# Gated feed-forward kernel: one unit of the up stage stays in PSUM, the product stage has 11 units instead of 12, and two roundings of the sigmoid move to POOL

## The chip, the cores and the metric

The program runs on one core of a Trainium2 chip. Times are device microseconds (us) of that core; lower is better. The kernel before was timed in three runs, and one further execution was recorded by the profiler. The words unit, half and bank are explained below.

## What is computed

Input are four sequences of 1024 tokens with 256 values each, a context of 154 rows for each sequence, and weights. After an attention block comes a feed-forward block with 768 hidden values, and it is this block that the change touches. All of its intermediate results are rounded to a grid whose step is the largest absolute value of the whole tensor divided by 32767, so that no rounding can start before the last value of its tensor is known:

```python
def act_qdq(x):
    scale = jnp.maximum(jnp.max(jnp.abs(x)) / qmax, 1e-12)
    return jnp.clip(jnp.round(x / scale), -qmax - 1.0, qmax) * scale
...
x = act_qdq(x)
up = act_qdq(x @ lpbq_dequant(w_up).T)
gate = act_qdq(x @ lpbq_dequant(w_gate).T)
sig = fixed_qdq_u16(jax.nn.sigmoid(gate))
gate = act_qdq(gate * sig)
o = act_qdq(gate * up)
return o @ lpbq_dequant(w_down).T
```

## The kernel before, in words

Every engine has its own list of instructions, written out by hand, and waits on semaphores (`wait_ge`) that other engines raise (`then_inc`). Nothing reorders them: the order in which the code is written is the order in which each engine works.

The hidden tensor is 768 x 4096 (hidden values x tokens). It is cut in 12 **units** of 128 hidden values x 2048 tokens; unit u has hidden block k = u // 2 and token half u % 2. PSUM is used as two halves, `ps[0]` and `ps[1]`, of four banks each; a unit fills one half, a bank takes 512 tokens. TensorE (PE) makes one unit with 24 matmuls (`hidden_unit`, lines 740 to 759): four banks, each from `xh` and `xl` (the high and low part of the rounded input) and the high and low weights. A unit may be started when the PSUM half is free (`half_free[0]`, `half_free[1]`), and `unit_ps` tells that it is complete.

The feed-forward block runs in four stages:

- **Gate stage.** PE makes the 12 gate units, ScalarE (ACT) copies them to `hid`, VectorE (DVE) takes the largest value. The overall largest gives scale 2.
- **Up stage.** PE makes the 12 up units, but only their largest value is taken (`up_max`, line 1450) and the unit is dropped, because the scale of `up` is not yet known and 12 more units in float32 have no room. In the same time the gate is worked on, unit by unit: integer gate `gq` (by ACT, POOL and once DVE), sigmoid and absolute value (ACT), the sigmoid rounded to 16 bits, `sq` (`sigmoid_int`: DVE for unit 0 and all odd units, POOL for the even ones from 2 on), and the product of both with its largest value (`gated_max`, line 1461, on DVE). At the end DVE forms scale 3 (of `up`) and scale 4 (of the gated gate). For both, POOL takes the largest value over the partitions (`over_all`, line 479).
- **Product stage.** PE makes the 12 up units a second time. For each, ACT writes the rounded absolute value `au` and the rounded gated value `pq`, and DVE multiplies the sign of the unit in PSUM into `gq` (`product_sign`, line 1486; it raises `half_free`) and multiplies `pq` and `au`, with the largest value (`product_max`, line 1493). The last unit is taken bank by bank and in two parts. Then DVE and POOL form scale 5.
- **Down stage.** 16 chunks of 256 tokens are rounded, split in high and low parts, multiplied with the down weights and added to the residual. 24 matmuls whose result is not used (`WARM`) run ahead of it while the last scale is formed.

What sets the order around the change: DVE works strictly through `up_max(u)`, the rounding of u where it is DVE's, `gated_max(u)`; POOL's rounding of unit u waits for `p_rdy` >= u, that is until `gated_max(u - 1)` is done, since it writes over `sq[0]`; `half_free` after `up_max` lets PE go on two units later. ACT's first `au` waits for scale 3, its first `pq` for scale 4. PE is always ahead by up to two units, as there are two PSUM halves.

The buffers `ag`, `sq[0]` and later `au`, `pq[0]` share one region of 12288 bytes, and `sq[1]` and `pq[1]` the region of the gate weights.

Of the kernel before, what the change touches and what calls it, by code (L numbers as in the profile page):

```python
# [38 lines left out]
P = 128  # L39
# [27 lines left out]
def build(nc, x, ctx, g_xattn, g_ffn, w_sim, b_sim, w_qv, b_qv, w_gate, w_up, w_down, out):  # L67
# [61 lines left out]
    au = place(a, "au", [P, 2, HALF], I16)  # L129
    pq = [place(a, "pq0", [P, HALF], I16), place(copy_of(r_wg), "pq1", [P, HALF], I16)]  # L130
# [56 lines left out]
    gmx, umx, pmx, omx = col(NU + 3), col(NU), col(NU), col(NU + 1)  # L187
# [25 lines left out]
    with ExitStack() as stack:  # L213
# [41 lines left out]
        gbank_ps, ubank0_ps, ubank_ps, aubank_rdy = map(sem, ("gbank_ps", "ubank0_ps", "ubank_ps", "aubank_rdy"))  # L255
# [34 lines left out]
        WARM = 24  # L290
        HC = P + D
# [20 lines left out]
        def down_ps(par):  # L312
            return ps[0][:, par * (CD // P):(par + 1) * (CD // P), 0:D]
# [19 lines left out]
        def _(sp):  # L333
# [21 lines left out]
            sp.wait_ge(unit_ps, 3 * NU)  # L355
# [25 lines left out]
        def _(pool):  # L381
# [115 lines left out]
            for u in range(2, NU, 2):  # L497
                sigmoid_int(u)
                if u + 3 < NU:
# [6 lines left out]
        def _(pe):  # L506
# [254 lines left out]
            def hidden(wh, wl, done, first, bank_ps, bank0_ps=None):  # L761

                with pe.Fori(0, KF - 1) as k:
# [56 lines left out]
            pe.wait_ge(half_free[0], 3 * KF + 1)  # L820
            for i in range(WARM):
                pe.matmul(ps[0][:, i % 4, :], wdh[:, 0, 0:P], wdl[:, 0:2, :].rearrange("p k n -> p (k n)"), start=True, stop=True)
# [11 lines left out]
        def _(act):  # L834
# [785 lines left out]
```

## Time and profile before

| what | value |
|---|---|
| median of 3 runs | 461.97 us (461.82 to 462.2) |
| profiled execution, its own time | 459.6 us |
| span of its profile, first to last instruction | 457.8 us |
| mean granted clock of PE | 0.992 of full speed |
| PE busy in the span | 433.4 us (95%) |
| DVE busy | 363.4 us (79%) |
| ACT busy | 274.6 us (60%) |
| POOL busy | 110.7 us (24%) |
| gate stage on PE ends at | 260.4 us |
| up stage on PE | 260.4 to 322.7 us |
| product stage on PE | 322.7 to 385.8 us |
| down stage, first real matmul to the end | 392.0 to 457.8 us |

How to read it: times within the profile count from the first instruction. A row of a timeline has the start, the duration, the engine, the line of the code, the operation with its output and input, and in brackets the idle time before it and who ended that. Instructions that follow each other at once on DVE or ACT overlap in the record by up to 0.1 us, so the pitch from start to start is a little shorter than the duration. The time beyond the span (459.6 against 457.8 us) lies around the first and the last instruction.

### The profile page before, as it was taken

Reading aid. Unit: us, or ns where it says so; the run is one execution under the profiler, and the core shown is the slowest. Engines: PE = TensorE matmul, PEld = TensorE weight load, DVE = VectorE, ACT = ScalarE, POOL = GpSimd, SP = SyncE. Lnnn points to the kernel's source line nnn. Section 1 sums busy time; section 2 is a strip of 40 time slices with the busy share of each in tenths; the row PEclk is TensorE's granted clock in tenths of the full one; section 3 lists DMA queues with packets and bytes.
Section 4 is the critical chain, followed back from the end, with each engine's and each line's share of the span. In section 5 each row is a group of like instructions: output and inputs, shape, how many; then the busy total and the mean of one; then the engine's idle time right before and its main releaser. Section 6 shows DMA issues by size and latency. Waiting matters only on the chain.

```text
span 457.8 us, 6771 instructions
## 1 busy us (share of the span) xinstructions
PE 433.4 (95%) x2432; PEld 297.2 (65%) x2432; DVE 363.4 (79%) x652; ACT 274.6 (60%) x346; POOL 110.7 (24%) x109
## 2 busy tenths in 40 slices
PE   4899999999997698999999999999999999999997
PEld 3788898889876586744444444444444444788886
DVE  6786789797777488886433789999998889898874
ACT  2677365556525023284334599999296779987760
POOL 1239274365744453100000013334100000000000
PEclk9999999999999799999999999999999999999999
DMA  7950002000200020110000000000000000344442
GB/s 242 314 166 0 1 2 92 1 0 3 92 1 0 0 94 0 43 50 0 0 0 0 1 1 1 0 0 0 1 0 0 0 0 0 117 139 139 137 137 70
DMA packets 20672, 21.13 MB, mean 46 GB/s; under 512 B 825, under 2 KB 20392, under 8 KB 20648
## 3 DMA queue, kind: packets, MB, share of 16 engines
q1 hardware_dynamic: 20628, 20.82, 14.4%
q8 instruction: 14, 0.23, 0.2%
q14 instruction: 10, 0.08, 0.1%
q10 hardware_dynamic: 20, 0.00, 0.0%
HBM read 12.43 MB, written 8.39 MB: 45 GB/s over the span
## 4 chain that ended last, share of the span: by engine, by line
PE 44%; DVE 24%; issue 19%; ACT 7%; POOL 4%; DMA 1%; ACTq 0%; POOLq 0%; DVEq 0%
PE ps L785 12%; PE ps L750 9%; PE ps L755 5%; DVE cols L1452 4%; DVE yb L1184 4%; PE ps L576 3%; PE ps L578 3%; PE ps L582 3%; DVE hid L1468 2%; ACT hid L1012 2%; PE ps L564 2%; PE ps L545 1%; PE ps L613 1%; POOL h L418 1%; ACT ag L1017 1%
## 5 line engine op out<-in xcount | busy, mean ns | idle before, releaser
L750 PE MATMUL ps<-xh,wuh 128*128 128x512 f16 x192 | 72.8, 379 | 0.8 <-DVE gq L1491 0.8
L750 PE MATMUL ps<-xh,wul 128*128 128x512 f16 x192 | 72.8, 379 | 0.0
L755 PE MATMUL ps<-xl,wuh 128*128 128x512 f16 x192 | 57.2, 379 | 0.0
L1431 DVE TENSOR_REDUCE cols<-hid x10 | 22.9, 2286 | 24.3 <-ACT hid L989 24.3
L785 PE MATMUL ps<-wdl,oh 128*128 128x256 f16 x168 | 37.4, 273 | 0.0
L785 PE MATMUL ps<-wdh,oh 128*128 128x256 f16 x168 | 37.4, 273 | 0.0
L750 PE MATMUL ps<-xh,wgl 128*128 128x512 f16 x96 | 36.4, 379 | 0.0
L750 PE MATMUL ps<-xh,wgh 128*128 128x512 f16 x96 | 36.4, 379 | 0.0
L989 ACT ACTIVATE hid<-ps 128x2048 f32 x10 | 18.8, 1875 | 27.5 <-PE ps L755 27.5
L750 PEld LDWEIGHTS ps<-xh,wuh 128*128 (+1 forms) x192 | 18.8, 98 | 24.0 <-issue 1.8
L482 POOL PARTITION_ALL_REDUCE cols<-cols x4 | 1.5, 374 | 135.0 <-DVE cols L1391 135.0
L755 PEld LDWEIGHTS ps<-xl,wuh 128*128 (+1 forms) x192 | 18.8, 98 | 22.7
L750 PEld LDWEIGHTS ps<-xh,wul 128*128 (+1 forms) x192 | 18.8, 98 | 22.4
L1184 DVE TENSOR_SCALAR yb<-xa,cols 128x256 f32<-128x256 f32 x30 | 23.7, 832 | 11.6 <-POOL cols L392 11.6
L564 PE MATMUL ps<-aT,cx 77*128 77x256 f32 x128 | 30.5, 381 | 0.0
L857 ACT ACTIVATE hT<-ps 128x512 f32<-128x512 f32 x16 | 9.4, 590 | 33.9 <-PE ps L531 33.9
L1491 DVE TENSOR_TENSOR gq<-gq,ps 128x2048 bf16<-128x2048 int16 x11 | 25.1, 2286 | 5.3 <-ACT au L1041 5.3
L1074 ACT ACTIVATE oq<-hid,cols 128x1536 int16 (+1 forms) x15 | 23.6, 1571 | 9.6 <-DVE ol L1547 9.6
L1468 DVE CUSTOM_DVE_ANT_0 hid<-ag,sq 128x2048 f32<-128x2048 int16 x12 | 29.1, 2424 | 0.2
L755 PE MATMUL ps<-xl,wgh 128*128 128x512 f16 x96 | 28.6, 379 | 0.1
L1452 DVE TENSOR_REDUCE cols<-ps 128x1 f32<-128x2048 f32 x12 | 27.4, 2286 | 1.6 <-PE ps L755 1.6
L576 PE MATMUL ps<-wv,hqT 128*128 128x256 f32 x104 | 27.7, 391 | 0.0
(223 smaller groups left out, 1039.8 us busy)
## 6 DMA issues: line engine op xcount, KB each, us to landing
x_scratch<-xa SPq DMA_DIRECT2D x4, 1024.0 KB, 4.4
xo<-x_scratch SPq DMA_DIRECT2D x16, 256.0 KB, 2.7
out_dram<-xo SPq DMA_DIRECT2D x15, 256.0 KB, 2.2
xa<-in_x SPq DMA_DIRECT2D x3, 1024.0 KB, 12.7
xa<-in_x SPq DMA_DIRECT2D x4, 256.0 KB, 4.5
wv<-in_L_xattn_W_qv SPq DMA_DIRECT2D x1, 1024.0 KB, 8.4
wr<-in_L_ffn_w_gate SPq DMA_DIRECT2D x1, 768.0 KB, 10.1
wr<-in_L_ffn_w_up SPq DMA_DIRECT2D x1, 768.0 KB, 11.5
```

What stands on the lines that cost most here:

```text
L564: mm = pe.matmul(hq_bank[:, d * PT:(d + 1) * PT], cx[b][0:JP, k, d * P:(d + 1) * P], aT[0:JP, n % 3, k, :], start=k == 0, stop=k == 1)
L576: pe.matmul(o_, hqT[:, par, d, q], wv[:, KD + d, :], start=d == 0, stop=False)
L750: pe.matmul(ps[hf][:, q, :], w_[:, d, ds(k * P, P)], xh[:, d, n], start=d == 0 and w_ is wh, stop=False)
L755: mm = pe.matmul(ps[hf][:, q, :], wh[:, d, ds(k * P, P)], xl[:, d, n], start=False, stop=d == KD - 1)
L785: mm = pe.matmul(down_ps(par)[:, t], o_[:, par, k, q], w_[:, k, :], start=not low and k == 0 and w_ is wdh, stop=low and k == KF - 1)
L989: act.activation(unit(hid, k, hf), ps_half(hf), ACT.Copy).then_inc(half_free[hf], 1)
L1074: act.activation(oq[:, par], hid[:, :, ds(c * CD, CD)], ACT.Copy, scale=c_co).then_inc(oqa_rdy, 1)
L1184: i_ = dve.tensor_scalar(yb[:, n % 2, t, :], xa[:, 2 * n + t, :], mv2[:, t, 0:1], rstd2[:, t:t + 1], ALU.subtract, ALU.mult)
L1431: dve.tensor_reduce(gmx[:, ds(k * 2 + hf, 1)], unit(hid, k, hf), AX.X, ALU.max, apply_absolute_value=True).then_inc(gm_done, 1)
L1452: dve.tensor_reduce(umx[:, u:u + 1], ps_half(u % 2), AX.X, ALU.max, apply_absolute_value=True).then_inc(half_free[u % 2], 1)
L1468: dve.tensor_tensor_reduce(half_of(hid, u), ag[:, u % 2, :], sq[u % 2][:], 1.0, 0.0, ALU.mult, ALU.max, pmx[:, u:u + 1]).then_inc(p_rdy, 1)
L1491: dve.tensor_tensor(g_.bitcast(BF16), g_, ps_half(hf), ALU.mult).then_inc(half_free[hf], 1)
```

## The change

- The last two units of the up stage are made in the other order: the second half of the tokens of block 5 (unit 11) goes to `ps[0]`, the first half (unit 10) to `ps[1]`. Unit 10 stays there. Its largest value is taken bank by bank (`kept_max`), and `half_free[1]` is not raised by it.
- When scale 3 is known, unit 10 is used out of `ps[1]`: DVE multiplies its sign in two parts (`kept_sign`), ACT writes `au` in two parts (`kept_up`), and only then `half_free[1]` is raised. `kept_product_max` multiplies it first of all.
- The product stage makes the 11 other units. The last is unit 11, now in `ps[0]`; the down stage and the warm matmuls use `ps[1]` instead of `ps[0]`.
- `SQ_POOL`: POOL rounds the sigmoid of units 2, 4, 6, 8, 9, 10 and 11, DVE that of 0, 1, 3, 5 and 7. Before, 9 and 11 were DVE's.
- Two DVE instructions that form constants (`c_ko`, `c_koq`) stand ahead of the first `product_sign` instead of behind it.
- `au` and `pq` are separate buffers in the same places.

The core of the diff:

```diff
+        SQ_POOL = [2, 4, 6, 8, 9, 10, 11]
...
-                pool.tensor_scalar(sq[0][:], half_of(hid, u), 65536.0, 1.0, ALU.mult, ALU.mult).then_inc(sqp_rdy, 1)
+                pool.tensor_scalar(sq[u % 2][:], half_of(hid, u), 65536.0, 1.0, ALU.mult, ALU.mult).then_inc(sqp_rdy, 1)
-            for u in range(2, NU, 2):
+            for u in SQ_POOL:
                 sigmoid_int(u)
-                if u + 3 < NU:
+                if u + 3 < NU and u % 2 == 0:
                     pool.wait_ge(p_rdy, u + 1)
...
-            def hidden_unit(k, hf, wh, wl, done, first, bank_ps=None):
+            def hidden_unit(k, hf, wh, wl, done, first, bank_ps=None, tokens=None):
...
-                    c = 4 * hf + q
+                    c = 4 * (hf if tokens is None else tokens) + q
...
-            def hidden(wh, wl, done, first, bank_ps, bank0_ps=None):
+                with pe.Fori(0, blocks - 1) as k:
                     for hf in range(2):
                         hidden_unit(k, hf, wh, wl, done, first)
-                hidden_unit(KF - 1, 0, wh, wl, done, first, bank0_ps)
-                hidden_unit(KF - 1, 1, wh, wl, done, first, bank_ps)
...
-            hidden(wgh, wgl, 0, True, gbank_ps)
-            hidden(wuh, wul, KF, False, None)
-            hidden(wuh, wul, 2 * KF, False, ubank_ps, ubank0_ps)
+            hidden(wgh, wgl, 0, True, KF)
+            hidden_unit(KF - 1, 0, wgh, wgl, 0, True)
+            hidden_unit(KF - 1, 1, wgh, wgl, 0, True, gbank_ps)
+            hidden(wuh, wul, KF, False, KF)
+            hidden_unit(KF - 1, 0, wuh, wul, KF, False, tokens=1)
+            hidden_unit(KF - 1, 1, wuh, wul, KF, False, mbank_ps, tokens=0)
+            hidden(wuh, wul, 2 * KF, False, KF - 1)
+            hidden_unit(KF - 2, 0, wuh, wul, 2 * KF, False)
+            hidden_unit(KF - 2, 1, wuh, wul, 2 * KF, False, ubank0_ps)
+            hidden_unit(KF - 1, 0, wuh, wul, 2 * KF, False, ubank_ps, tokens=1)
...
-            def first_up(u):
-                act.wait_ge(scales, 3)
-                act.wait_ge(unit_ps, 2 * NU + u + 1)
-                act.wait_ge(p_rdy, NU - 1 + u)
-                act.activation(au[:, u, :], ps_half(u), ACT.Abs, scale=c_cu).then_inc(au_rdy, 1)
+            def kept_up(part):
+                n = slice(part * HALF // 2, (part + 1) * HALF // 2)
+                act.wait_ge(kept_sgn, part + 1)
+                return act.activation(au[1][:, n], ps[1][:, 2 * part:2 * part + 2, :].rearrange("p a n -> p (a n)"), ACT.Abs, scale=c_cu)
             def product_int(k, hf):
-                ge(act, o_rdy, k * 2 + hf - 1)
+                act.wait_ge(o_rdy, k * 2 + hf)
                 act.activation(pq[hf][:], unit(hid, k, hf), ACT.Copy, scale=c_cp).then_inc(pq_rdy, 1)
             def up_int(k, hf):
                 act.wait_ge(unit_ps, 2 * NU + k * 2 + hf + 1)
                 plain(act)
-                act.activation(au[:, hf, :], ps_half(hf), ACT.Abs, scale=c_cu).then_inc(au_rdy, 1)
-            first_up(0)
+                act.activation(au[hf][:], ps_half(hf), ACT.Abs, scale=c_cu).then_inc(au_rdy, 1)
+            act.wait_ge(scales, 3)
+            act.wait_ge(p_rdy, NU - 1)
+            kept_up(0)
+            kept_up(1).then_inc(half_free[1], 1)
+            act.wait_ge(unit_ps, 2 * NU + 1)
+            act.activation(au[0][:], ps_half(0), ACT.Abs, scale=c_cu).then_inc(au_rdy, 1)
             act.wait_ge(scales, 4)
+            act.activation(pq[1][:], half_of(hid, NU - 2), ACT.Copy, scale=c_cp).then_inc(pq_rdy, 1)
             act.activation(pq[0][:], half_of(hid, 0), ACT.Copy, scale=c_cp).then_inc(pq_rdy, 1)
-            first_up(1)
+            act.wait_ge(unit_ps, 2 * NU + 2)
+            act.wait_ge(o_rdy, 1)
+            act.activation(au[1][:], ps_half(1), ACT.Abs, scale=c_cu).then_inc(au_rdy, 1)
             act.activation(pq[1][:], half_of(hid, 1), ACT.Copy, scale=c_cp).then_inc(pq_rdy, 1)
-            with act.Fori(1, KF - 1) as k:
+            with act.Fori(1, KF - 2) as k:
                 for hf in range(2):
                     product_int(k, hf)
                     up_int(k, hf)
...
+            def kept_max(q):
+                dve.wait_ge(mbank_ps if q < 3 else unit_ps, q + 1 if q < 3 else 2 * NU)
+                dve.tensor_reduce(umx[:, NU - 1 + q:NU + q], ps[1][:, q, :], AX.X, ALU.max,
+                                  apply_absolute_value=True).then_inc(um_done, 1)
...
-            for u in range(NU):
+            for u in range(NU - 1):
                 up_max(u)
-                if u == NU - 1:
-                    dve.wait_ge(half_free[1], 2 * KF + 1)
-                    largest(2, (half_free[0], 2 * KF + 1), umx)
-                if u == 0 or u % 2 == 1:
+                if u not in SQ_POOL:
                     sigmoid_int(u)
-                if u == NU - 1:
-                    v = overall(2)
-                    link(dve.tensor_scalar(c_su, v, c_kuq, EPS, ALU.mult, ALU.max))
-                    link(dve.reciprocal(c_ru, c_su))
-                    dve.tensor_scalar(c_cu, c_ru, c_ku, None, ALU.mult).then_inc(scales, 1)
                 gated_max(u)
-            largest(3, (p_rdy, NU), pmx)
+            for q in range(4):
+                kept_max(q)
+            dve.wait_ge(um_done, 4)
+            largest(2, (half_free[0], 2 * KF + 1), umx)
...
+            def kept_sign(part):
+                n = slice(part * HALF // 2, (part + 1) * HALF // 2)
+                g_ = half_of(gq, NU - 2)[:, n]
+                dve.tensor_tensor(g_.bitcast(BF16), g_, ps[1][:, 2 * part:2 * part + 2, :].rearrange("p a n -> p (a n)"),
+                                  ALU.mult).then_inc(kept_sgn, 1)
+            def kept_product_max():
+                dve.wait_ge(half_free[1], 2 * KF + 1)
+                dve.wait_ge(pq_rdy, 1)
+                dve.tensor_tensor_reduce(half_of(hid, NU - 2), pq[1][:], au[1][:], 1.0, 0.0,
+                                         ALU.mult, ALU.max, omx[:, 0:1]).then_inc(o_rdy, 1)
...
+            kept_sign(0)
+            v = overall(2)
+            link(dve.tensor_scalar(c_su, v, c_kuq, EPS, ALU.mult, ALU.max))
+            link(dve.reciprocal(c_ru, c_su))
+            dve.tensor_scalar(c_cu, c_ru, c_ku, None, ALU.mult).then_inc(scales, 1)
+            kept_sign(1)
+            gated_max(NU - 1)
+            largest(3, (p_rdy, NU), pmx)
             v = overall(3)
             link(dve.tensor_scalar(c_sp, v, c_kpq, EPS, ALU.mult, ALU.max))
             link(dve.reciprocal(c_rp, c_sp))
             dve.tensor_scalar(c_cp, c_rp, c_kp, None, ALU.mult).then_inc(scales, 1)
-            for u in range(NU - 1):
+            link(dve.tensor_scalar(c_ko, c_su, c_sp, None, ALU.mult))
+            link(dve.tensor_scalar(c_koq, c_ko, 1.0 / QMAX, None, ALU.mult))
+            for u in range(NU - 2):
                 product_sign(u)
                 if u == 0:
-                    link(dve.tensor_scalar(c_ko, c_su, c_sp, None, ALU.mult))
-                    link(dve.tensor_scalar(c_koq, c_ko, 1.0 / QMAX, None, ALU.mult))
+                    kept_product_max()
                 product_max(u)
```

POOL (GpSimd), the end of its work in the up stage, before. `sq` is the rounded sigmoid, L492 its rounding; L482 with `cols` is the all-reduce for scales 2 to 5, here the last three; the L482 row without operands is an instruction that the compiler puts where POOL changes from one kind of operation to the other:

```order
L486 TENSOR_SCALAR gq<-hid,cols 128x2048 [waits p_rdy]
L492 TENSOR_SCALAR sq_62<-hid 128x2048 [waits p_rdy,sig_rdy]
L486 TENSOR_SCALAR gq<-hid,cols 128x2048 [waits p_rdy]
L492 TENSOR_SCALAR sq_62<-hid 128x2048 [waits p_rdy,sig_rdy]
L482 ISA
L482 ISA cols<-cols 128x1 [waits loc_rdy] x3
```

The same place with the change:

```order
L488 TENSOR_SCALAR gq<-hid,cols 128x2048 [waits p_rdy]
L494 TENSOR_SCALAR sq_63<-hid 128x2048 [waits p_rdy,sig_rdy]
L494 TENSOR_SCALAR sq_62<-hid 128x2048 [waits p_rdy,sig_rdy]
L494 TENSOR_SCALAR sq_63<-hid 128x2048 [waits p_rdy,sig_rdy]
L484 ISA
L484 ISA cols<-cols 128x1 [waits loc_rdy] x3
```

Two roundings more stand between the last integer gate and the row without operands, and all three of the last roundings wait for DVE's products (`p_rdy`). The same kind of row stands once more, in both kernels, between the first all-reduce and the first integer gate.

DVE, from the last maximum of the up stage to the first product, before (L1391 collects the columns for a scale, L1459 is the rounding of unit 11, L1468 the product `gated_max`, L1480 to L1482 form scale 3, L1511 to L1513 scale 4):

```order
L1452 TENSOR_REDUCE cols<-ps 128x1 [waits unit_ps]
L1391 TENSOR_REDUCE cols<-cols 128x1 [waits half0_free,half1_free]
L1459 TENSOR_SCALAR sq_63<-hid 128x2048 [waits p_rdy,sig_rdy]
L1480 TENSOR_SCALAR cols<-cols 128x1 [waits all_rdy]
L1481 RECIPROCAL cols<-cols 128x1 [waits chain]
L1482 TENSOR_SCALAR cols<-cols 128x1 [waits chain]
L1468 ISA hid,cols<-ag,sq_63 128x2048 [waits ag_rdy,sqv_rdy]
L1468 ISA cols 128x1
L1391 TENSOR_REDUCE cols<-cols 128x1 [waits p_rdy]
L1511 TENSOR_SCALAR cols<-cols 128x1 [waits all_rdy]
L1512 RECIPROCAL cols<-cols 128x1 [waits chain]
```

With the change (L1472 is `kept_max`, L1517 `kept_sign`, L1493 `gated_max`):

```order
L1472 TENSOR_REDUCE cols<-ps 128x1 [waits mbank_ps] x3
L1472 TENSOR_REDUCE cols<-ps 128x1 [waits unit_ps]
L1410 TENSOR_REDUCE cols<-cols 128x1 [waits half0_free,um_done]
L1517 TENSOR_TENSOR gq<-gq,ps 128x1024
L1546 TENSOR_SCALAR cols<-cols 128x1 [waits all_rdy]
L1547 RECIPROCAL cols<-cols 128x1 [waits chain]
L1548 TENSOR_SCALAR cols<-cols 128x1 [waits chain]
L1517 TENSOR_TENSOR gq<-gq,ps 128x1024
L1493 ISA hid,cols<-ag,sq_63 128x2048 [waits ag_rdy,sqp_rdy]
L1493 ISA cols 128x1
L1410 TENSOR_REDUCE cols<-cols 128x1 [waits p_rdy]
L1553 TENSOR_SCALAR cols<-cols 128x1 [waits all_rdy]
```

The wait for the all-reduce of scale 3 (`all_rdy`) now stands ahead of the second `kept_sign` and of the last `gated_max`, as it stood ahead of the last `gated_max` before; no rounding lies under it any more.

## Rows read from the trace of the kernel before

**Rows 1.** Busy by stretch: length, then each engine (count), PE clock, DMA.

```profile
265.00:323.00 58.00, 58.00 (x270) 26.20 (x269) 56.96 (x38) 54.80 (x29) 19.52 (x10) 1.00 0.00 0
334.00:387.00 53.00, 52.98 (x246) 24.15 (x247) 47.60 (x35) 43.22 (x29) 0.00 (x0) 1.00 0.00 0
```

**Rows 2.** Timeline of DVE, end of the up stage, first product.

```profile
313.49 0.08 DVE L1468 DVE_READ_ACCUMULATOR2_ANT cols<- 128x1 f32 x1
...
316.94 2.29 DVE L1468 CUSTOM_DVE_ANT_0 hid<-ag,sq 128x2048 f32<-128x2048 int16 x1
...
325.89 0.17 DVE L1391 TENSOR_REDUCE cols<-cols 128x1 f32<-128x12 f32 x1
325.97 1.23 DVE L1459 TENSOR_SCALAR sq<-hid 128x2048 uint16<-128x2048 f32 x1
...
327.92 0.21 DVE L1482 TENSOR_SCALAR cols<-cols 128x1 f32<-128x1 f32 x1
...
331.48 0.21 DVE L1513 TENSOR_SCALAR cols<-cols 128x1 f32<-128x1 f32 x1
331.61 2.27 DVE L1491 TENSOR_TENSOR gq<-gq,ps 128x2048 bf16<-128x2048 int16 x1
```

**Rows 3.** Timeline of POOL around the up stage.

```profile
261.62 0.38 POOL L482 PARTITION_ALL_REDUCE cols<-cols  x1 [67.78 <-DVE cols L1391]
268.96 2.14 POOL L486 TENSOR_SCALAR gq<-hid,cols 128x2048 int16<-128x2048 f32 x1 [6.96 <-issue]
...
313.67 1.97 POOL L486 TENSOR_SCALAR gq<-hid,cols 128x2048 int16<-128x2048 f32 x1 [2.45 <-DVE cols L1468]
319.40 1.90 POOL L492 TENSOR_SCALAR sq<-hid 128x2048 uint16<-128x2048 f32 x1 [3.77 <-DVE cols L1468]
327.02 0.42 POOL L482 PARTITION_ALL_REDUCE cols<-cols  x1 [5.72 <-DVE cols L1391]
330.64 0.35 POOL L482 PARTITION_ALL_REDUCE cols<-cols  x1 [3.20 <-DVE cols L1391]
```

**Rows 4.** Chain of waits: start, duration, what; before POOL's second all-reduce.

```profile
326.07 0.96 issue
```

**Rows 5.** Timeline of DVE beside POOL's first integer gate.

```profile
268.05 1.22 DVE L1459 TENSOR_SCALAR sq<-hid 128x2048 uint16<-128x2048 f32 x1
269.30 3.94 DVE L1468 CUSTOM_DVE_ANT_0 hid<-ag,sq 128x2048 f32<-128x2048 int16 x1
```

**Rows 6.** Timeline of PE: product stage, its stall, its end.

```profile
322.71 0.38 PE L750 MATMUL ps<-xh,wuh 128*128 128x512 f16 x1
...
334.02 0.39 PE L750 MATMUL ps<-xh,wuh 128*128 128x512 f16 x1 [0.79 <-DVE gq L1491]
...
385.83 5.34 PE L822 MATMUL ps<-wdl,wdh 128*128 128x512 f16 x24
```

**Rows 7.** Timeline of ACT, product stage.

```profile
331.72 2.00 ACT L1045 ACTIVATE pq<-hid,cols 128x2048 int16<-128x2048 f32 x1 [1.59 <-DVE cols L1513]
...
344.68 1.97 ACT L1041 ACTIVATE au<-ps,cols 128x2048 int16<-128x2048 f32 x1 [1.33 <-PE ps L755]
```

**Rows 8.** Timelines of DVE and ACT: shorter passes.

```profile
257.62 1.28 DVE L1437 TENSOR_REDUCE cols<-ps 128x1 f32<-128x512 f32 x2
...
399.81 1.21 DVE L1534 TENSOR_TENSOR gq<-gq,ps 128x1024 bf16<-128x1024 int16 x1
...
261.31 0.60 ACT L995 ACTIVATE hid<-ps 128x512 f32<-128x512 f32 x1 [0.23 <-DVE cols L1437]
```

**Rows 9.** Timeline of DVE: end of the last product.

```profile
388.87 0.08 DVE L1507 DVE_READ_ACCUMULATOR2_ANT cols<- 128x1 f32 x1
```

**Rows 10.** Timeline of PE after its longest wait.

```profile
152.54 1.01 PE L648 MATMUL ps<-ones,h 128*128 128x1 f32 x4 [6.49 <-POOL h L435]
```

**Rows 11.** PE by stretch: length, busy (count), granted clock, DMA, GB/s.

```profile
150.00:151.00 1.00, 0.00 (x0) 0.60 0.00 0
157.00:158.00 1.00, 1.00 (x6) 0.98 0.00 0
```

More of the change, by code:

```diff
@@ L353, in _ @@
             sp.wait_ge(x1_out, 16 * B)
-            sp.wait_ge(unit_ps, 3 * NU)
+            sp.wait_ge(unit_ps, 3 * NU - 1)
             sp.wait_ge(o_rdy, NU + 1)
@@ L759, in hidden_unit, with hidden @@
                 mm.then_inc(unit_ps, 1)
-            def hidden(wh, wl, done, first, bank_ps, bank0_ps=None):
-                with pe.Fori(0, KF - 1) as k:
+            def hidden(wh, wl, done, first, blocks):
+                with pe.Fori(0, blocks - 1) as k:
                     for hf in range(2):
                         hidden_unit(k, hf, wh, wl, done, first)
-                hidden_unit(KF - 1, 0, wh, wl, done, first, bank0_ps)
-                hidden_unit(KF - 1, 1, wh, wl, done, first, bank_ps)
             pe.wait_ge(wt_rdy, 9)
-            hidden(wgh, wgl, 0, True, gbank_ps)
-            hidden(wuh, wul, KF, False, None)
-            hidden(wuh, wul, 2 * KF, False, ubank_ps, ubank0_ps)
+            hidden(wgh, wgl, 0, True, KF)
[8 more added lines that the diff above has]
+            hidden_unit(KF - 1, 0, wuh, wul, 2 * KF, False, ubank_ps, tokens=1)
             def down(c, par):
@@ L818, in down_last @@
                     mm.then_inc(dnl_ps if t == 0 else dn_ps, 1)
-            pe.wait_ge(half_free[0], 3 * KF + 1)
+            pe.wait_ge(half_free[1], 3 * KF)
             for i in range(WARM):
-                pe.matmul(ps[0][:, i % 4, :], wdh[:, 0, 0:P], wdl[:, 0:2, :].rearrange("p k n -> p (k n)"), start=True, stop=True)
+                pe.matmul(ps[1][:, i % 4, :], wdh[:, 0, 0:P], wdl[:, 0:2, :].rearrange("p k n -> p (k n)"), start=True, stop=True)
             down_first()
@@ L1051, in _ @@
                     up_int(k, hf)
-            product_int(KF - 1, 0)
+            product_int(KF - 2, 0)
+            up_int(KF - 2, 0)
+            product_int(KF - 2, 1)
             for q in range(4):
-                act.wait_ge(ubank0_ps if q < 3 else unit_ps, q + 1 if q < 3 else 3 * NU - 1)
-                a_ = act.activation(au[:, 0, bank_of(q)], ps[0][:, q, :], ACT.Abs, scale=c_cu)
+                act.wait_ge(ubank0_ps if q < 3 else unit_ps, q + 1 if q < 3 else 3 * NU - 2)
+                a_ = act.activation(au[1][:, bank_of(q)], ps[1][:, q, :], ACT.Abs, scale=c_cu)
             a_.then_inc(au_rdy, 1)
-            product_int(KF - 1, 1)
+            act.wait_ge(o_rdy, NU - 2)
+            act.activation(pq[0][:], half_of(hid, NU - 1), ACT.Copy, scale=c_cp).then_inc(pq_rdy, 1)
             for q in range(4):
-                act.wait_ge(ubank_ps if q < 3 else unit_ps, q + 1 if q < 3 else 3 * NU)
-                act.activation(au[:, 1, bank_of(q)], ps[1][:, q, :], ACT.Abs,
+                act.wait_ge(ubank_ps if q < 3 else unit_ps, q + 1 if q < 3 else 3 * NU - 1)
+                act.activation(au[0][:, bank_of(q)], ps[0][:, q, :], ACT.Abs,
                                scale=c_cu).then_inc(aubank_rdy if q < 3 else au_rdy, 1)
@@ L1065, in gate_sign @@
                 act.activation(sg, sg, ACT.Sign).then_inc(sgn_rdy, 1)
-            act.wait_ge(half_free[0], 3 * KF + 1)
+            for hf in range(2):
+                act.wait_ge(half_free[hf], 3 * KF)
             gate_sign(0)
@@ L1527, in _ @@
             link(dve.tensor_scalar(c_fin, c_so, c_ft, None, ALU.mult))
-            dve.wait_ge(half_free[0], 3 * KF + 1)
+            for hf in range(2):
+                dve.wait_ge(half_free[hf], 3 * KF)
             def last_product_sign(part):
```

31 lines of the change are left out of this document (16 added, 15 removed).

## Prediction, made before the changed kernel ran

> **What bounds the kernel now.** I read the busy time by stretch first. In the up stage PE is busy for all of 58.00 us and DVE for 56.96; in the product stage PE for 52.98 of 53, DVE for 47.60 [rows 1]. Both stages run at PE's pace, and in the up stage DVE is so full that one more microsecond on it is a delay. The timeline of PE gives the product stage: first matmul at 322.71, one stall of 0.79 us before 334.02, then nothing until the warm matmuls at 385.83 [rows 6]. From 334.02 ten units take 51.81 us, so a unit is 5.18 us. DVE ends its last product 3.12 us after that, at 388.95 [rows 9], and the down stage follows. So a shorter kernel needs an earlier end of PE's product stage, and that end is: start of the first unit that had to wait, plus 5.18 us for each unit from there.
>
> The wait belongs to the scales. Scale 3 is there at 328.13, scale 4 at 331.69, and DVE's first sign product starts behind it at 331.61 [rows 2]; PE runs its two free PSUM halves and then needs that product. What makes scale 3 late stands in the timeline of POOL [rows 3]. DVE has the local maximum at 326.06 [rows 2], but POOL's all-reduce starts at 327.02; the next one starts at 330.64, 0.1 us after its own maximum. The chain of waits has 0.96 us there as "issue" [rows 4]. Before that all-reduce stands the row without operands that the order of POOL shows, and the same row stands before the first integer gate. There POOL was idle for 6.96 us, from 262.00 to 268.96, and the row names "issue", no semaphore; here it was idle for 5.72 us, from 321.30 [rows 3]. I read both as the time of that row: **changing POOL's program costs 5.7 to 7.0 us, counted from the end of POOL's last operation**, and nothing before it in its queue can be skipped.
>
> **The change, part by part.** The sum is against the profiled execution's own times.
>
> 1. *Rounding of unit 9 by POOL.* DVE's product of unit 8 is complete at 313.57 and POOL starts its last integer gate at 313.67, for 1.97 us [rows 2, 3]. The rounding of unit 9 queues behind that: 315.67 to 317.57, at 1.90 us. DVE's product of unit 9 starts at 317.60 instead of 316.94 [rows 2]: +0.66. DVE saved its own rounding of 1.2 us there but waits for it longer.
> 2. *Rounding of units 10 and 11.* After the product of 9 (2.2 us from start to start, 319.89 with its result) POOL rounds unit 10 from 320.05 to 321.95 while DVE takes the maximum; DVE multiplies unit 10 from 322.02 and is done at 324.30. Only then may POOL round unit 11: 324.46 to 326.36. Before, POOL's last rounding started at 319.40 and ended at 321.30 [rows 3]. POOL's last operation thus ends 5.06 us later.
> 3. *The four bank maxima* of the kept unit: two take 1.28 us [rows 8], four some 2.5, so 324.22 to 326.7; the local maximum is ready at 326.9. This is hidden by POOL, as is the first half of the sign product, 1.21 us [rows 8].
> 4. *The program change now starts at 326.36.* With 5.72 us the all-reduce starts at 332.08, takes 0.42, and scale 3 is there 0.7 us later, at 333.19: **+5.06**. DVE stands in order behind it with the second sign half and the product of unit 11, and is idle from about 328 to 332.5. That idle time costs because both are needed.
> 5. *Scale 4.* DVE: second sign half 333.11 to 334.32, product of unit 11 to 336.53, then the maximum, an all-reduce without a change of program, three small instructions: scale 4 at 337.88, 4.69 us after scale 3 where it was 3.56; the difference is the sign half ahead of it. `c_ko` and `c_koq` move forward by 0.4 us ahead of the first sign product.
> 6. *ACT reads the kept half out of PSUM*, 1024 columns twice. No row has this size: 512 columns take 0.60 and 2048 take 1.97 [rows 7, 8]; between them I take 1.06. The second starts after the second sign half and ends at 335.42. Then `ps[1]` is free and PE may start its second unit at 335.56. Its first ended at 322.71 + 5.18 = 327.89, so **PE is idle for 7.67 us** where it had 0.96.
> 7. *The clock.* The one wait of that kind in the trace is 6.49 us before 152.54 [rows 10]. In it the granted clock fell during 150 to 151, from full to the half level (1.2 of 2.4 GHz), and it was back at full only from 157.0, some 4.5 us after the matmuls began again [rows 11]. I take the same here: 4.5 us at half speed are 2.24 us of work lost. The second unit ends at 342.98.
> 8. *One unit less.* Nine units remain: 342.98 + 9 x 5.18 = 389.60 against 385.83. Nothing else stalls PE if this holds: DVE's sign product of unit 1 starts at 345.3 and frees its half at 347.7, PE needs it at 348.16; the next frees at 353.33 for 353.34. The kept product adds 2.2 us to DVE once and lies beside PE's slow unit. The tail of 3.12 us stays: DVE's end moves with PE's end.
>
> Sum at the end of PE's product stage: +7.68 (second unit starts at 335.56, not 327.88), +2.24 clock, -0.96 (stall that is gone before the third unit), -5.18 (one unit less) = **+3.8 us**. Nothing in the down stage changes but the PSUM half. The profiled execution takes 459.6 us, 2.4 below the median of 461.97; I put the difference on the median: **465.8 us**. The saved unit is real; it pays for a scale that comes 5 us late and for a cold restart.
>
> **A rule against my reading.** DVE's own rounding at 325.97 lasts until 327.20 and covers the 0.96 us [rows 2]. On the other hand POOL's gate at 268.96 did start while such a rounding ran (268.05 to 269.27), and it was DVE's next product that became 3.94 us long instead of 2.29 [rows 2, 3, 5]: overlap shows in durations, not in a late start. So I keep the program change as the cause. The Trainium skill (SBUF — State Buffer, "SBUF: two separate sides") says that DVE and GpSimd share a port pair under an exclusive lock, so that the loser blocks fully. By that rule the 0.96 us could be DVE's rounding alone; the sum would be the first rival's. The Trainium skill (GPSIMD Engine Reference, "Instruction dispatch") says on the other side that the first call of newly loaded code pays about 6 us with no visible instruction; a sum with 6 us would come to +4.1, and the 6.96 and 5.72 us of the trace agree with it.
>
> **Rivals.**
>
> - *The program change is hidden (faster).* If it is short and the 0.96 us had another cause, the all-reduce starts at 327.04, scale 3 is at 328.66, PE waits 3.1 us at its second unit, which is less than the wait that cost the clock, and ends at 384.53: -1.3, **460.7 us**. It decides below 2.5 us of program change; from there on the change loses. For it: only the overlap in time. Against: the 6.96 us that nothing else explains. Up to 4.86 us the program change would have stayed hidden before (321.30 to 326.16), so that is its upper bound under this rival: +2.4. Chance of the fast end 0.08, of the stretch between 0.05.
> - *The clock stays at full.* The halts are alike but not equal. Then the second unit ends at 340.74, and DVE is what stalls PE (1.34 us before the fourth unit, 0.37 before the fifth): 389.07, +3.25, **465.2 us**. Chance 0.17.
> - *The program change takes 6.96 us*, as in the other direction: +5.0, **467.0 us**. Chance 0.12.
> - *The clock stays low longer.* Lost 3.2 to 4.5 us instead of 2.24: +4.8 to +6.1, **466.7 to 468 us**. Chance 0.10.
>
> **How the numbers follow.** My forecast keeps 0.48; it and the rivals that lose sum to 0.87. The range runs from 464.2 (program change 4.7 us, full clock) to 467.4 (6.96 us with half a microsecond more of low clock); outside are the hidden case, most of the stretch above it and the longest low clock, together about 0.18. A measurement tells 0.2% from no change, 0.92 us here. Faster by that needs a program change under about 1.5 us: 0.07. Within it (1.5 to 3.4 us): 0.03. Slower: 0.90.
>
> **What would show it.** POOL: last rounding ends near 326.4, next all-reduce near 332.1, with some 5.7 us idle. DVE: idle about 4.5 us between the first sign half and scale 3. PE: a wait of 7 to 8 us before its second product unit, granted clock at half for some microseconds after it, product stage ends near 389.6. Wrong would be: an all-reduce at 327 (first rival), a wait of PE below 4 us, or an end of PE's product stage before 385.

## The result, and the profile after

The changed kernel takes **465.78 us** (median of 6 runs, 463.73 to 467.11); the kernel before took 462.09 us (median of 6). The ratio is **1.0086**, 95% interval 1.0045 to 1.0128: slower. The forecast was 465.8 us. Medians here and below count every execution, while the ratios leave out the few that took far longer (760.31, 512.92 and 917.45 us of the kernel before, 905.82 us of the run in which scale 3 has no all-reduce).

| what | before | after |
|---|---|---|
| profiled execution, its own time | 459.6 us | 467.11 us |
| span of its profile | 457.8 us | 465.3 us |
| mean granted clock of PE | 0.992 | 0.974 |
| PE busy in the span | 433.4 us (95%) | 432.0 us (93%) |
| POOL busy | 110.7 us (24%) | 114.4 us (25%) |
| DVE's first up maximum | 265.84 | 269.30 |
| first warm matmul (end of PE's product stage) | 385.83 | 393.32 |
| **stretch between these two** | **119.99 us** | **124.02 us** |

The profiled execution of after is 7.5 us longer, twice what the medians show. 3.46 us of that lie ahead of the change: the attention block, which is the same code, ended that much later, with PE's mean granted clock at 0.93 between 100 and 200 us against 0.97. I therefore compare all kernels over one stretch, from DVE's first up maximum to the first warm matmul. It holds all that the change touches but the PSUM half of the down stage, and grew by 4.03 us. A time "in the stretch" counts from DVE's first up maximum. Each stretch comes from the one profiled execution of its kernel, each ratio from all its runs.

POOL's timeline of after, which answers to [rows 3]:

```profile
272.51 2.05 POOL L488 TENSOR_SCALAR gq<-hid,cols 128x2048 int16<-128x2048 f32 x1 [7.05 <-issue]
...
317.12 1.97 POOL L488 TENSOR_SCALAR gq<-hid,cols 128x2048 int16<-128x2048 f32 x1 [2.45 <-DVE cols L1493]
319.06 1.90 POOL L494 TENSOR_SCALAR sq<-hid 128x2048 uint16<-128x2048 f32 x1
323.45 1.90 POOL L494 TENSOR_SCALAR sq<-hid 128x2048 uint16<-128x2048 f32 x1 [2.50 <-DVE cols L1493]
327.85 1.90 POOL L494 TENSOR_SCALAR sq<-hid 128x2048 uint16<-128x2048 f32 x1 [2.51 <-DVE cols L1493]
335.59 0.38 POOL L484 PARTITION_ALL_REDUCE cols<-cols  x1 [5.84 <-issue]
```

The roundings of units 9, 10 and 11 stand one behind the other with DVE's products between them. After the last, POOL does nothing for 5.84 us. The row without operands has a name in the record of POOL's queue, `MODIFY_POOL_CONFIG`, and a time: 329.9, some 0.2 us after the last rounding's end. In the kernel before it was at 321.5, with the last rounding ending at 321.30 and the local maximum ready only at 326.06. So it is taken up as soon as the operation before it ends, and does not wait for the maximum. DVE's side, which answers to [rows 2]:

```profile
316.94 0.08 DVE L1493 DVE_READ_ACCUMULATOR2_ANT cols<- 128x1 f32 x1
...
320.99 2.29 DVE L1493 CUSTOM_DVE_ANT_0 hid<-ag,sq 128x2048 f32<-128x2048 int16 x1 [1.76 <-POOL sq L494]
...
327.62 2.47 DVE L1472 TENSOR_REDUCE cols<-ps 128x1 f32<-128x512 f32 x4
330.13 0.17 DVE L1410 TENSOR_REDUCE cols<-cols 128x1 f32<-128x15 f32 x1
330.21 1.21 DVE L1517 TENSOR_TENSOR gq<-gq,ps 128x1024 bf16<-128x1024 int16 x1
336.00 0.21 DVE L1546 TENSOR_SCALAR cols<-cols 128x1 f32<-128x1 f32 x1 [4.58 <-POOL cols L484]
...
336.45 0.21 DVE L1548 TENSOR_SCALAR cols<-cols 128x1 f32<-128x1 f32 x1
336.58 1.21 DVE L1517 TENSOR_TENSOR gq<-gq,ps 128x1024 bf16<-128x1024 int16 x1
...
341.14 0.21 DVE L1555 TENSOR_SCALAR cols<-cols 128x1 f32<-128x1 f32 x1
```

The local maximum is ready at 330.30. DVE fills 1.2 us with the first sign half, then waits 4.58 us. The chain of waits, where [rows 4] had 0.96, now has

```profile
330.31 5.29 issue
```

ACT cannot write `au` of the kept unit before scale 3, so PSUM half 1 stays taken and PE stops. ACT, then PE, which answers to [rows 6]:

```profile
336.70 2.24 ACT L1038 ACTIVATE au<-ps,cols 128x1024 int16<-128x1024 f32 x2 [11.47 <-DVE cols L1548]
```

```profile
339.00 0.61 PE L752 MATMUL ps<-xh,wuh 128*128 128x512 f16 x1 [7.48 <-ACT au L1038]
...
344.09 0.40 PE L752 MATMUL ps<-xh,wuh 128*128 128x512 f16 x1
...
346.70 0.38 PE L752 MATMUL ps<-xh,wuh 128*128 128x512 f16 x1
```

The matmuls behind 339.00 come every 0.43 us (339.39, 339.82, 340.25), those behind 344.09 every 0.22: half speed for 5.1 us. The second unit ends at 346.70. PE by stretch (length, busy (count), granted clock, DMA, GB/s) says the same:

```profile
332.00:334.00 2.00, 0.00 (x0) 0.97 0.00 0
334.00:336.00 2.00, 0.00 (x0) 0.50 0.00 0
...
342.00:344.00 2.00, 2.00 (x6) 0.50 0.00 0
344.00:346.00 2.00, 2.00 (x10) 0.97 0.00 0
```

The granted clock was at full (2.4 GHz) while PE worked, fell to half (1.2 GHz) near 334 with PE at rest since about 331.5, and came back at 344.1. The group of matmuls with which each unit of the up and product stages begins has all its waiting in this one place:

```profile
L752 PE MATMUL ps<-xh,wuh 128*128 128x512 f16 x184 | 70.8, 385 | 7.5 <-ACT au L1038 7.5
```

### The profile page after: what moved, and what is told of

The parts are those of the page before. It is cut to its first block, busy times and chain, and to the rows that moved or that the text cites. A ratio compares the mean times of both kernels' runs of the same rounds, so it can differ in the third digit from the quotient of the medians.

```text
span 465.3 us, 6718 instructions
## 1 busy us (share of the span) xinstructions
PE 432.0 (93%) x2408; PEld 296.5 (64%) x2408; DVE 361.3 (78%) x654; ACT 274.8 (59%) x347; POOL 114.4 (25%) x111
## 4 chain that ended last, share of the span: by engine, by line
PE 43%; DVE 23%; issue 20%; ACT 7%; POOL 5%; DMA 1%; ACTq 0%; POOLq 0%; DVEq 0%
PE ps L792 12%; PE ps L752 9%; PE ps L757 4%; DVE yb L1203 4%; DVE cols L1477 3%; PE ps L578 3%; PE ps L580 3%; PE ps L584 3%; DVE hid L1493 2%; ACT hid L1019 2%; PE ps L566 1%; PE ps L547 1%; PE ps L615 1%; POOL h L420 1%; ACT ag L1024 1%
## 5 line engine op out<-in xcount | busy, mean ns | idle before, releaser
L752 PE MATMUL ps<-xh,wuh 128*128 128x512 f16 x184 | 70.8, 385 | 7.5 <-ACT au L1038 7.5
L752 PE MATMUL ps<-xh,wul 128*128 128x512 f16 x184 | 70.8, 385 | 0.0
L757 PE MATMUL ps<-xl,wuh 128*128 128x512 f16 x184 | 55.6, 384 | 0.0
L1493 DVE CUSTOM_DVE_ANT_0 hid<-ag,sq 128x2048 f32<-128x2048 int16 x12 | 29.1, 2423 | 1.9 <-POOL sq L494 1.8
L580 PE MATMUL ps<-wv,prT 128*128 128x256 f32 x104 | 27.6, 389 | 0.0
L394 POOL TENSOR_TENSOR cols<-cols 128x2 f32<-128x2 f32 x15 | 11.6, 775 | 64.6 <-DVE cols L1197 64.6
```

The costliest lines, as they stand in the source:

```text
L580: pe.matmul(o_, prT[:, par, d, q], wv[:, 2 * KD + d, :], start=False, stop=False)
L752: pe.matmul(ps[hf][:, q, :], w_[:, d, ds(k * P, P)], xh[:, d, n], start=d == 0 and w_ is wh, stop=False)
L757: mm = pe.matmul(ps[hf][:, q, :], wh[:, d, ds(k * P, P)], xl[:, d, n], start=False, stop=d == KD - 1)
L1493: dve.tensor_tensor_reduce(half_of(hid, u), ag[:, u % 2, :], sq[u % 2][:], 1.0, 0.0, ALU.mult, ALU.max, pmx[:, u:u + 1]).then_inc(p_rdy, 1)
```

## The experiments

Two theories. **A:** POOL's change of program, nearly 6 us counted from its last rounding, sets scale 3; the two roundings moved it back by 5 us. **B:** the kept unit costs too much around the scales (four maxima, sign halves, PSUM half taken longer) and would lose without the roundings too.

Each ratio is against the kernel before, timed on the same chip in the same session, with 4 to 12 runs of each variant.

### The kept unit alone

Units 9 and 11 are rounded by DVE again; the rest is the changed kernel.

```diff
-        SQ_POOL = [2, 4, 6, 8, 9, 10, 11]
+        SQ_POOL = [2, 4, 6, 8, 10]
...
             kept_sign(1)
+            sigmoid_int(NU - 1)
             gated_max(NU - 1)
```

> The kept unit without the two moved roundings: POOL rounds only units 2, 4, 6, 8 and 10, DVE rounds 11 between the second sign half and the last product of the up stage. Theory (POOL's program change, 5.7 to 5.8 us counted from its last rounding, is what made scale 3 late): the last rounding ends as in the kernel before, the all-reduce starts as there, scale 3 is as early as before (62.3 us after DVE's first maximum of the up stage), scale 4 some 2.4 us later than before because of the sign halves. PE waits 2.6 us at its second product unit, and from DVE's first maximum of the up stage to the warm matmuls it takes 119.4 us (before: 120.0): 461.5 us. Rival (the kept unit itself is what costs, by its sign halves, its two ACT passes and the extra product ahead of the first): it stays 2 us or more above the kernel before, over 464.

461.23 us, ratio 0.9985 (0.9971 to 0.9999), stretch 119.75.

```profile
329.82 0.38 POOL L484 PARTITION_ALL_REDUCE cols<-cols  x1 [5.81 <-DVE cols L1410]
```

```profile
333.23 0.61 PE L752 MATMUL ps<-xh,wuh 128*128 128x512 f16 x1 [2.46 <-ACT au L1038]
```

The all-reduce is at 61.47 in the stretch, where it was at 61.18 before and at 66.29 in after. PE waits 2.46 us instead of 7.48. Theory B falls: the kept unit pays for itself. It gains only a quarter of a microsecond of 5.18, because PE still waits for scale 3, the clock fell here too (0.50 between 334 and 336), and PE stalls twice more for DVE's sign products, 0.73 us before 346.14 and 0.34 before 351.83.

### The roundings alone

The kernel before, with units 9 and 11 rounded by POOL as in the change.

```diff
+        SQ_POOL = [2, 4, 6, 8, 9, 10, 11]
...
-            for u in range(2, NU, 2):
+            for u in SQ_POOL:
```

> The kernel before with the roundings of units 9 and 11 moved to POOL, and twelve product units as before. Theory: POOL's last rounding ends 5.06 us later, the program change follows, scale 3 comes 5.06 us later, PE waits 6 us before its third product unit instead of 1, and it is then PE alone that sets the end: 125.0 us from DVE's first maximum to the warm matmuls if the clock stays up, 127.3 if it falls in that wait as in the changed kernel: 467 to 469.4 us. Rival (the kept unit is the cost, the roundings relieve DVE): as the kernel before or below, 120.0 us in that stretch.

468.46 us, ratio 1.0131 (1.0079 to 1.0183), stretch 126.75: **+6.8 us**.

```profile
324.95 1.90 POOL L493 TENSOR_SCALAR sq<-hid 128x2048 uint16<-128x2048 f32 x1 [2.50 <-DVE cols L1469]
332.83 0.38 POOL L483 PARTITION_ALL_REDUCE cols<-cols  x1 [5.98 <-issue]
```

```profile
339.80 0.60 PE L751 MATMUL ps<-xh,wuh 128*128 128x512 f16 x1 [4.81 <-DVE gq L1492]
```

The last rounding ends at 326.85, the local maximum is ready at 327.21, and the all-reduce starts 5.6 us later. PE waits 4.81 us, not the expected 6, since the all-reduce is at 65.07 in the stretch instead of 66.24: DVE was faster in the up stage of this execution (the last section has the reason). All of the loss is here; the kept unit gave part of it back: it takes 0.24 us off without the roundings (119.99 to 119.75) and 2.73 with them (126.75 to 124.02).

### Scale 3 without its all-reduce

The changed kernel, but each partition takes its own maximum for scale 3, and POOL's all-reduce for it is left out. The other work is the same.

```diff
-            for n in range(2, 5):
+            for n in range(3, 5):
                 over_all(n)
...
-                dve.wait_ge(all_rdy, n)
+                if n == 2:
+                    dve.wait_ge(loc_rdy, 2)
+                    return c_loc[:, 2:3]
+                dve.wait_ge(all_rdy, n if n == 1 else n - 1)
```

> The changed kernel without POOL's all-reduce for scale 3: each partition takes its own largest value as scale 3 (so the result differs from the reference), all else as in the changed kernel, both roundings on POOL included. The program change then lies between the last rounding and the all-reduce of scale 4, which is needed only some 5.8 us after that rounding, so it is just hidden. Theory: scale 3 comes 4.5 us earlier than in the changed kernel, PE waits 3.1 us at its second product unit, 118.7 us from DVE's first maximum to the warm matmuls: 460.7 us. Rival (waits of DVE's rounding for POOL and the kept unit's passes are the cost, not the program change): 122 us or more in that stretch, over 464.

460.02 us, ratio 0.9968 (0.9937 to 0.9998), stretch 118.72, which is 5.3 less than after. Scale 3 starts with the first sign half's end, at 328.15. The program change now lies ahead of scale 4 and beside DVE's product: the next all-reduce starts at 332.47, 5.92 us after the last rounding and 0.13 after DVE's local maximum for scale 4. It was therefore hidden, as expected, and its own length can't be read in this run. PE waits 2.81 us, and the clock fell all the same:

```profile
331.13 0.39 PE L752 MATMUL ps<-xh,wuh 128*128 128x512 f16 x1 [2.81 <-ACT au L1038]
```

```profile
332.00:334.00 2.00, 2.00 (x6) 0.50 0.00 0
```

### PE kept at work through the wait

The changed kernel; the last bank of the first product unit is computed five more times.

```diff
-                for q in range(4):
+                for q in list(range(4)) + [3] * again:
...
+            hidden_unit(0, 0, wuh, wul, 2 * KF, False, again=5)
```

> The changed kernel, but the last bank of the first product unit is computed six times instead of once (6.5 us of matmuls that give the same values), so that PE is at work while it would wait for the kept half. Theory (the lost clock makes PE late at its second unit, DVE's queue takes over when it is not): granted clock at full throughout, the second unit 5.2 us long, PE stalls about 1.3 and 0.4 us before the fourth and the fifth unit, and the stretch from DVE's first maximum to the warm matmuls is 0.5 to 0.8 us shorter than in the changed kernel: 465.1 us. Rival (the slow unit is hidden behind DVE and ACT): the same stretch as in the changed kernel within 0.1 us.

464.36 us, ratio 1.0054 (1.0035 to 1.0074), stretch 123.70. The granted clock stays at 1.00.

```profile
337.19 0.39 PE L752 MATMUL ps<-xh,wuh 128*128 128x512 f16 x1 [1.25 <-ACT au L1042]
...
348.86 0.39 PE L752 MATMUL ps<-xh,wuh 128*128 128x512 f16 x1 [1.13 <-DVE gq L1515]
...
354.54 0.39 PE L752 MATMUL ps<-xh,wuh 128*128 128x512 f16 x1 [0.33 <-DVE gq L1515]
```

The half clock cost 2.5 us of PE's work, but keeping it at full gives back only 0.3: two new stalls, 1.13 and 0.33 us, appear where DVE's sign product is now the slower one, and scale 3 came 0.4 us later in the stretch (the program change took 6.08 us). So in the stretch the low clock is worth 0.3 to 0.7 us. The late scale is the main part: even at full clock this kernel is 3.95 us above the kept unit alone (123.70 against 119.75). By the ratios the gain is about 1.5 us, but their intervals overlap (1.0045 to 1.0128 and 1.0035 to 1.0074).

### What were the 0.96 us of before?

The prediction put them on the program change alone, against a rule that DVE's own rounding could be the cause. Three variants of the kernel before separate the two. In the first, unit 10 is rounded by DVE, so that POOL's last operation lies nearly 12 us back:

```diff
+        SQ_POOL = [2, 4, 6, 8]
```

> The kernel before, but unit 10 is rounded by DVE as well, so that POOL's last operation is the integer gate of unit 11 and ends 5.7 us earlier. Theory (the 0.96 us between DVE's local maximum and POOL's all-reduce are the rest of the program change): the all-reduce starts 0.1 us after the local maximum, as the next two do, although DVE's rounding of unit 11 still runs beside it. Rival (that rounding of DVE holds POOL back): it starts 0.9 to 1.0 us after the local maximum as before. Either way DVE has one rounding more, 1.2 us, and scale 3 comes 0.5 to 1 us later: about 121 us from DVE's first maximum to the warm matmuls, 463 us.

463.6 us, ratio 1.0025 (0.9997 to 1.0053), stretch 121.25. POOL, then DVE:

```profile
330.33 1.24 POOL L483 PARTITION_ALL_REDUCE cols<-cols  x1 [11.82 <-DVE cols L1392]
334.77 0.35 POOL L483 PARTITION_ALL_REDUCE cols<-cols  x1 [3.20 <-DVE cols L1392]
```

```profile
330.02 0.17 DVE L1392 TENSOR_REDUCE cols<-cols 128x1 f32<-128x12 f32 x1
330.11 1.23 DVE L1460 TENSOR_SCALAR sq<-hid 128x2048 uint16<-128x2048 f32 x1
```

The all-reduce starts at once, 0.14 us after the local maximum (ready at 330.19), but takes 1.24 us instead of 0.35 and ends at 331.57, 0.23 us after DVE's rounding. Scale 3 comes no earlier after its maximum than before: 331.57 - 330.19 = 1.38 us, and 327.44 - 326.06 = 1.38 in [rows 2, 3]. There too the all-reduce ended 0.24 us after DVE's rounding (327.44 and 327.20).

The second also moves DVE's rounding of unit 11 behind scale 3 (its forecast calls that rounding an operation of "DVE's two-sided kind"); the third moves only that, and leaves unit 10 to POOL. The diff is that of the second; in the third the condition still reads `u == 0 or u % 2 == 1`.

```diff
                 up_max(u)
...
-                if u not in SQ_POOL:
-                    sigmoid_int(u)
                 if u == NU - 1:
                     v = overall(2)
...
                     dve.tensor_scalar(c_cu, c_ru, c_ku, None, ALU.mult).then_inc(scales, 1)
+                if u not in SQ_POOL:
+                    sigmoid_int(u)
                 gated_max(u)
```

> The kernel before with unit 10 rounded by DVE (so that POOL is idle long before the late all-reduce) and with DVE's rounding of unit 11 moved behind scale 3 (so that nothing of DVE's two-sided kind runs beside the all-reduce). If the all-reduce with unit 10 on DVE took 1.24 us because DVE's rounding ran beside it, it now starts 0.1 to 0.2 us after the local maximum and takes 0.35 to 0.42: the first constant of scale 3 starts 0.6 to 0.9 us after the local maximum instead of 1.4. If instead the first all-reduce after a program change is long by itself, it takes 1.2 us again. Either way DVE's rounding now stands between the scales: scale 4 comes 0.3 to 0.5 us later than with unit 10 on DVE alone, the stretch from DVE's first up maximum to the warm matmuls is 121.6 us (121.25 there), the ratio near 1.003.

> The kernel before with only DVE's rounding of unit 11 moved behind scale 3; POOL still rounds unit 10. If the program change is what held the all-reduce there, it starts again 5.7 to 6.1 us after POOL's last rounding, 0.9 to 1.3 us after the local maximum, and takes 0.38 us; scale 3 comes as before, scale 4 and the end of the product stage 1.1 to 1.3 us later, stretch 121.2 us, ratio 1.002 to 1.004. If DVE's rounding alone held it, the all-reduce starts 0.1 to 0.2 us after the local maximum, scale 3 comes 0.6 us sooner, the stretch is 120.6 us.

463.66 us, ratio 1.0039 (1.0024 to 1.0054), stretch 120.56; and 463.85 us, ratio 1.0038 (1.0025 to 1.0051), stretch 123.35. POOL in the one and in the other:

```profile
328.46 0.38 POOL L483 PARTITION_ALL_REDUCE cols<-cols  x1 [12.09 <-DVE cols L1392]
```

```profile
321.71 1.90 POOL L492 TENSOR_SCALAR sq<-hid 128x2048 uint16<-128x2048 f32 x1 [3.76 <-DVE cols L1468]
329.77 0.38 POOL L482 PARTITION_ALL_REDUCE cols<-cols  x1 [6.16 <-issue]
```

With both away the all-reduce starts 0.13 us after the maximum and takes 0.38. With only the rounding away it starts 6.16 us after POOL's last rounding, 1.40 us after the maximum. So in the kernel before **two causes ended within 0.2 us of each other**: the program change at 327.02, DVE's rounding at 327.20. Taking either away gains nothing. (In the third the all-reduce even came 0.4 us later after its maximum, because the program change was longer in that execution.) The third variant is longer than expected (121.2) in two known parts: the program change took 6.16 us where 5.72 was the case before, and PE's wait of 2.45 us brought the clock down (0.50 between 340 and 342), which cost 1.7 us between scale 4 and the warm matmuls. The second came out 1.0 us short of its expected 121.6; the last section has the likely cause. By their medians the two kernels differ by only 0.2 us: the profiled execution of the second was the shortest of its ten runs (462.3 us), that of the third the longest (465.29), so the gap of 2.8 us between their stretches is one of executions, not of kernels.

### Versions that might beat both

From the kept unit alone: the kept unit's maximum in one pass, and the two constants behind the first product again.

```diff
-            for q in range(4):
-                kept_max(q)
-            dve.wait_ge(um_done, 4)
+            kept_max()
+            dve.wait_ge(um_done, 1)
```

> The kept unit alone as in the first experiment, with the maximum of the kept unit in one pass instead of four (all its banks are complete by then) and the two constants formed behind the second product instead of ahead of the first sign product. Theory (with the program change out of the way, DVE's order between scale 4 and the third product is what is left): 0.4 us less than the first experiment, 119.3 us from DVE's first maximum to the warm matmuls, 460.9 us. Rival (PE's slow second unit hides it): as the first experiment, 119.75 us.

461.34 us, ratio **0.9977** (0.9959 to 0.9996), stretch 118.32. And with one bank of the first product unit computed once more (`again=1`):

> The kernel of e6_even_late_constants with the last bank of the first product unit computed twice, 1.3 us of matmuls, so that PE's wait before its second unit is 1.2 us instead of 2.5. Theory (in the first experiment the clock fell in a wait of 2.46 us and the slow second unit cost some 0.3 us): clock at full throughout, 119.0 us from DVE's first maximum to the warm matmuls, 460.7 us. Rival (the slow unit ends before its result is wanted): the stretch of e6_even_late_constants within 0.1 us.

461.09 us, ratio **0.9978** (0.996 to 0.9997), stretch 118.15. Both beat both kernels; against the kernel before it is about 1 us. The second edit had nothing to prevent in the profiled execution: PE's wait in the first is 1.74 us and the granted clock stayed at 1.00. Its stretch is 0.17 us shorter, which is neither the 0.3 of its theory nor the 0.1 of the rival. In both, PE later stalls 0.60 and 1.69 or 1.70 us for DVE's sign products. That these two are better than the kept unit alone is not shown: the intervals overlap, and about 1 us of their shorter stretch is the collision that the last section tells of.

## Why the prediction was right

The time, the sign and the mechanism came out. Step by step, in the stretch (predicted times less 265.84, measured less 269.30):

1. *Unit 9's rounding.* The product of unit 9 starts 4.05 us after that of unit 8 is complete (316.94 to 320.99). Predicted 313.49 to 317.60, 4.11.
2. *Units 10 and 11.* POOL's last rounding ends at 60.45; predicted 60.52.
3. *Four bank maxima* took 2.47 us, predicted 2.5; local maximum at 61.00, predicted 61.06. Hidden, as said.
4. *Program change.* 5.84 us where 5.72 was taken; all-reduce at 66.29, predicted 66.24. Scale 3 ready at 67.36, predicted 67.35.
5. *Scale 4* at 72.05, predicted 72.04; 4.69 us after scale 3, as predicted.
6. *ACT and PE's wait.* The second unit starts at 69.70, predicted 69.72. The wait is 7.48 us against 7.67. The estimate for 1024 columns (1.06 us) holds within 0.1: the second pass ends 1.15 us after the second sign half.
7. *The clock.* This term was mis-sized, by 0.3 us: 5.1 us at half speed lose 2.5 us, against 4.5 and 2.24. The one earlier case [rows 10, 11] fell and rose over other matmuls.
8. *Nine units* took 393.32 - 346.70 = 46.62 us, 5.18 each, with no stall between. DVE's tail is 3.14 us (396.46), predicted 3.12.

Sum: +4.03 us, predicted +3.8; the difference is step 7. That the median met the forecast within 0.1 us owes something to chance: the spread of the runs is over 3 us, and the 2.4 us that the forecast added for the difference between the profiled execution and the median are an offset of one execution of the kernel before.

The reasons beside the sum did less well in three places.

- *"So I keep the program change as the cause"* of the 0.96 us was half of it. The rounding of DVE would have held the all-reduce until the same moment. The sum did not suffer, because in the change no rounding of DVE runs beside the all-reduce and the program change alone decides. The remark that overlap shows in durations and not in a late start was borne out: 1.24 us instead of 0.35. The Trainium skill (SBUF — State Buffer, "SBUF: two separate sides") says that the loser of the port lock blocks fully; the unit-10-by-DVE run agrees, its all-reduce ended 0.23 us after DVE's rounding. But it did not follow from that rule that scale 3 would be free of POOL's program change: both hold at once.
- *Rival 1* said that a wait of 3.1 us "is less than the wait that cost the clock". Waits of 2.45, 2.46 and 2.81 us cost it in the runs. Its time would have stood all the same: the run without the all-reduce, with a wait of 2.81 us, is close to its case, and has a stretch of 118.72 us where the rival's end at 384.53 makes 118.69. The rival's sum has 1.7 us between the start of the second unit and the end that its ten units at 5.18 us do not fill, which is what it gives for stalls behind DVE at full clock (1.34 and 0.37); in the run it was the low clock that took 1.9 us there, and no stall followed. The number was right for another reason than the one given.
- *Rival 2* (clock at full, +3.25, stalls of 1.34 and 0.37) was worked out right: with PE kept at work the stalls were 1.13 and 0.33, and the stretch +3.7, of which 0.4 is the later scale 3. It did not happen by itself.

The program change as a rival of 6.96 us did not occur in this direction: it took 5.72 to 6.16 us in the kernel before, in after and in the six experiments that show it (5.81, 5.98, 6.08, 6.02, 5.85, 6.16; in the other three it was over before the all-reduce was wanted), and 6.9 to 7.7 us in the other direction, before the first integer gate. The Trainium skill (GPSIMD Engine Reference, "Instruction dispatch") gives about 6 us for the first call of newly loaded code; all these runs agree within 0.3 us for the all-reduce.

## What to carry to other kernels

In these kernels POOL paid 5.7 to 6.2 us for a change of program, counted from the end of its last operation, so the last operation of the old kind is what has to be early, not the first of the new; giving such an engine "free" work just ahead of a short step on the critical path can cost more (6.8 us here) than a saved unit of PE's work is worth (5.18). A short gap that the chain calls "issue" may have two causes that end together: take away one and look whether the gap moves, before counting on it. And a saved unit of work on the bounding engine is only worth what the scale behind it lets through.

## What was not expected of the hardware

- **The clock falls in shorter waits than the kernel before showed.** There the wait was 6.49 us [rows 10]. In these runs PE worked without a pause before each wait, with these results: waits of 1.25, 1.52, 1.74 and 2.05 us left the granted clock at 1.00; waits of 2.45, 2.46, 2.81, 4.81 and 7.48 us were followed by matmuls at half speed. In the run with 2.81 us the first matmul after the wait still took 0.39 us, and the clock was at 0.50 in the next 2 us; in the one with 2.45 us PE had been back at work for over a microsecond (from 337.99) when it fell between 339 and 340. The low time after the restart was 3.4 to 5.9 us. Each wait was seen in one execution only. With the kept unit alone the mean granted clock of the whole span was 0.981 in the profiled execution and 0.985 to 0.989 in eight of the nine others, so the fall may belong to some executions and not to all.
- **Which engine loses a collision changes from execution to execution, and it moves the whole up stage.** POOL's first integer gate and DVE's first product start within 0.43 us of each other. Where POOL is first, DVE's product takes 3.94 us [rows 5] to 4.15; where DVE is first, it takes 2.29 and POOL's gate takes 3.8 to 4.05 instead of 2. (Of starts less than 0.1 us apart, as in the run with the kept unit alone, the records don't tell which was first; the durations do.) DVE and POOL in the run with the roundings alone:

```profile
271.21 2.29 DVE L1469 CUSTOM_DVE_ANT_0 hid<-ag,sq 128x2048 f32<-128x2048 int16 x1
```

```profile
271.30 4.05 POOL L487 TENSOR_SCALAR gq<-hid,cols 128x2048 int16<-128x2048 f32 x1 [7.38 <-issue]
```

In the profiled executions DVE was the later one before, after, with the kept unit alone, without the all-reduce, with PE kept at work, with unit 10 by DVE and with only the rounding moved; POOL was the later one with the roundings alone, in both last versions and with both causes away. The four of the second kind have a local maximum for scale 3 that comes 1.0 to 1.4 us earlier in the stretch than in their nearest relative of the first. Which it is goes with the length of POOL's program change before that gate (6.87 to 7.34 us where POOL was first, 7.38 to 7.67 where DVE was). That this also makes part of the spread between runs is likely but not measured.
